# A decoder on one core: W2's butterflies moved from the experts to the second attention, and the experts' down weights split by VectorE

## The reference

```
x = x + L0_attn(layernorm(x)); x = x + L0_graph(ctx, layernorm(x))
x = x + moe(layernorm(x))               # 32 experts, capacity 256 rows
    gu  = rows_e @ w_gate_up[e]         # 256 x 512 @ 512 x 512
    act = silu(gu[:, :256]) * gu[:, 256:]
    y   = act @ w_down[e]               # 256 x 256 @ 256 x 512, gathered back per token by its gate
x = x + self_attention(layernorm(x)); x = x + cross_attention(layernorm(x), ctx)
x = x + ffn(layernorm(x))
    h   = silu(x @ W1.T) * (x @ W3.T)   # 2048 hidden features
    out = hadamard(h) @ W2.T            # Walsh-Hadamard transform over the 2048 hidden features
```

## Time and profile before

| what | value |
|---|---|
| median of 3 runs | 2982.72 us (2970.9 to 2985.78) |
| profiled execution, its own time | 2978.98 us |
| its span, first to last instruction | 2977.2 us |
| mean granted TensorE clock | 0.91 |
| busy, share of the span | PE 84%, PEld 55%, DVE 60%, ACT 41%, POOL 28% |

### The profile page before, as it was taken

How to read it: one execution, slowest core, us unless ns; L and a number is a source line. 1 busy time by engine, 2 the same in 40 slices (tenths; PEclk the granted TensorE clock), 3 DMA queues, 4 the chain that set the end, 5 groups by cost and what they waited for, 6 DMA issues and landing times. The chain is left out here.

```text
span 2977.2 us, 34561 instructions
## 1 busy us (share of the span) xinstructions
PE 2487.6 (84%) x12822; PEld 1650.5 (55%) x12822; DVE 1776.5 (60%) x2764; ACT 1224.9 (41%) x1859; POOL 833.9 (28%) x1064
## 2 busy tenths in 40 slices
PE   5898989874443458888859999999999879999999
PEld 4454545422222248778744554545655448888887
DVE  3766666636799956777736555555565444444443
ACT  3443444326767624444404333433433223333332
POOL 2222223214567637888700000001221110000000
PEclk8999999985666679999979999999999989999999
DMA  3313132203232348999842322334433432101000
GB/s 112 73 44 85 44 86 47 71 25 98 79 106 79 126 167 219 261 250 254 193 107 72 86 79 68 100 82 107 115 98 90 120 111 81 43 1 43 1 29 15
DMA packets 177289, 287.62 MB, mean 97 GB/s; under 512 B 20785, under 2 KB 52401, under 8 KB 177138
## 3 DMA queue, kind: packets, MB, share of 16 engines
q1 hardware_dynamic: 159730, 250.25, 28.4%
q0 software_dynamic: 14336, 34.61, 5.8%
q10 hardware_dynamic: 3072, 0.79, 0.1%
HBM read 149.79 MB, written 59.51 MB: 70 GB/s over the span
## 5 line engine op out<-in xcount | busy, mean ns | idle before, releaser
L657 DVE TENSOR_REDUCE at_negmax<-at_ps 128x2 f32<-128x1024 f32 (+3 forms) x256 | 259.2, 1017 | 131.2 <-PE at_ps L420 66.6
L572 ACT ACTIVATE at_probs<-at_ps 128x1024 f32<-128x1024 f32 (+3 forms) x256 | 221.8, 866 | 264.7 <-PE at_ps L440 262.1
L1258 DVE TENSOR_REDUCE a_negmax<-a_ps 128x2 f32<-128x1024 f32 x128 | 155.1, 1217 | 135.8 <-PE a_ps L1011 135.2
L50 PE MATMUL ff_ps<-ff_xnT_hi,ff_s_hi 128*128 128x512 f32 x512 | 201.0, 393 | 5.1 <-DVE ff_xnT_lo L2750 5.1
L52 PE MATMUL ff_ps<-ff_xnT_hi,ff_s_lo 128*128 128x512 f32 x512 | 200.2, 391 | 0.0
L51 PE MATMUL ff_ps<-ff_xnT_lo,ff_s_hi 128*128 128x512 f32 x512 | 200.1, 391 | 0.0
L1841 ACT ACTIVATE gr_act_signs<-gr_signed,gr_test 128x512 bf16<-128x512 f32 x248 | 177.3, 717 | 25.0 <-POOL gr_test L2204 13.4
L1159 ACT ACTIVATE a_probs<-a_ps 128x1024 f32<-128x1024 f32 x128 | 130.9, 1024 | 136.0 <-PE a_ps L1029 135.5
L2780 DVE TENSOR_TENSOR ff_hid<-ff_hid,ff_ps 128x512 f32<-128x512 f32 x64 | 44.0, 688 | 238.7 <-ACT ff_hid L2725 238.7
L440 PE MATMUL at_ps<-at_qk 98*128 98x512 f32 (+3 forms) x512 | 171.7, 417 | 17.4 <-DMA at_qk<-at_mrow 10.9
L50 PE MATMUL ex_ps<-ex_x_hi,ex_gu_hi 128*128 128x256 f32 x512 | 150.8, 294 | 35.7 <-issue 35.7
(11 more groups left out here) (411 smaller groups left out, 6503.3 us busy)
## 6 DMA issues: line engine op xcount, KB each, us to landing
at_qk<-at_part SPq DMA_DIRECT2D x384, 128.0 KB, 2.3
first_gu<-in_L_ffn_w_gate_up_dram SPq DMA_DIRECT2D x32, 1024.0 KB, 5.9
a_qk<-a_part SPq DMA_DIRECT2D x192, 128.0 KB, 2.3
first_d<-in_L_ffn_w_down_dram SPq DMA_DIRECT2D x32, 512.0 KB, 7.0
gr_aside_raw<-in_L_ffn_W_dram SPq DMA_DIRECT2D x48, 256.0 KB, 3.3
w13T<-gr_aside_out SPq DMA_DIRECT2D x32, 256.0 KB, 3.3
shared_x<-x_after_cross SPq DMA_DIRECT2D x8, 1024.0 KB, 8.0
ff_slab<-w13T SPq DMA_DIRECT2D x14, 512.0 KB, 6.9
```

The lines of the kernel that those rows point to most:

```text
L50: pe.matmul(out, lh, rh, start=start, stop=False, skip_group_check=True)
L572: act.activation(probs[:, t % 2, 2 * w:2 * w + 2, lo:S], banks(("kq", g, s), lo), ACT.Exp, scale=SCALE).then_inc(free(("kq", g, s)), 1)
L657: dve.reduce_max(negmax[:, g % 2, :].rearrange("p (j t) -> p j t", t=NT)[:, 2 * w:2 * w + 2, t], banks(("qk", g, s), 0, width(g, t)), AX.X ...
L1258: dve.reduce_max(negmax[:, g % 2, :].rearrange("p (j t) -> p j t", t=NT)[:, 2 * w:2 * w + 2, t], banks(("qk", g, s)), AX.X, negate=True).t ...
```

## The change

- The loads, butterflies and stores of W2 leave `experts`. In `attention_layers` they come back in 16 tiles of 32 columns (`MIX_COLS = HD`): at the end of SP's work of step g (g = 0 to 16) SP stores tile g-1 and loads tile g, 256 KB each in runs of 128 bytes, 2048 runs a transfer; in Pool's iteration g (1 to 16), ahead of oT(g-1), Pool does the 8 halves of tile g-1, each 128x256. `load_for_network` waits for the last store.
- `d_lo` is made by VectorE, right behind its y, and no longer by Pool.
- The order of the last two experts: both hidden parts (SiLU, h_hi; hid, h_lo) come ahead of both results on ScalarE and VectorE.

```diff
@@ attention_layers, SP
+            def load_w2(n):
+                if n:
+                    sp.wait_ge(mixed, 2 * MIX_STAGES * n)
+                sp.dma_start(mix[:, n % 2, :].rearrange("p (k c) -> p k c", c=MIX_COLS), w2_tiles[n]).then_inc(w2_in, 16)
+            def store_w2(n):
+                sp.wait_ge(mixed, 2 * MIX_STAGES * (n + 1))
+                sp.dma_start(mixed_tiles[n], mix[:, n % 2, :].rearrange("p (k c) -> p k c", c=MIX_COLS)).then_inc(w2_out, 16)
...
                 if has(g + 3):
                     stack(g + 3)
+                n = g - MIX_AT
+                if 0 <= n < MIX_TILES:
+                    store_w2(n)
+                if 0 <= n + 1 < MIX_TILES:
+                    load_w2(n + 1)
@@ attention_layers, Pool
+            def butterfly(n, stage, half):
...
+                        pool.wait_ge(w2_in, 16 * (n + 1))
+                        if n:
+                            pool.wait_ge(w2_out, 16 * n)
+                    if n or stage:
+                        pool.wait_ge(mixed, 2 * (MIX_STAGES * n + stage))
+                pool.tensor_tensor((c, d)[half], a, b, (ALU.add, ALU.subtract)[half]).then_inc(mixed, 1)
...
+                if 0 <= g - MIX_AT < MIX_TILES:
+                    for s in range(2 * MIX_STAGES):
+                        butterfly(g - MIX_AT, s // 2, s % 2)
                 if has(g - 1):
                     pool.wait_ge(rec_done, NT * g)
@@ experts, VectorE
+            def split_d(i, u):
+                d_hi_done[u].wait(dve, i, 1)
+                low(flat(d_lo[:, u]), flat(raw_d[:, u]), flat(d_hi[:, u]), d_lo_done[u])
...
+                if more:
+                    split_d(i + 1, u)
-                butterfly(e)
+            for e in range(E_ROUTED - 2):
+                hidden(e // 2, e % 2, True)
+                result(e // 2, e % 2, True)
+            for u in range(2):
+                hidden(PAIRS - 1, u, False)
+            for u in range(2):
+                result(PAIRS - 1, u, False)
@@ experts, Pool
-            split_d(0, 0)
-            split_d(0, 1)
...
-                if e + 2 < E_ROUTED:
-                    split_d(e // 2 + 1, e % 2)
```

More of the change, by code:

```diff
@@ L2258, with experts @@
 I_DIM = 256
-def experts(nc, env, tag, normed, index, target, sums, w_gate_up, w_down, w2T, w2_mixed, raw_gu, raw_d, shared_x, shared_rows):
+def experts(nc, env, tag, normed, index, target, sums, w_gate_up, w_down, raw_gu, raw_d, shared_rows):
     F = 2 * I_DIM // P
@@ L2412, in split_x, with hidden @@
                 act.copy(flat(x_hi[:, u]), flat(ps[:, 0:2, :])).then_inc(x_hi_done[u].sem, 1)
-            def body(i, u, more):
+            def hidden(i, u, more):
                 gu_ready[u].wait(act, i, 1)
@@ L2421, in body, with result @@
                     split_gu(i + 1, u)
+            def result(i, u, more):
                 y_ready[u].wait(act, i, 1)
@@ L2465, in body @@
                 dve.tensor_scalar(y[:, u, 1, :], ps[:, 7, :], gates[:, 2 * i + u, 1:2], None, ALU.mult).then_inc(y_dve[u].sem, 1)
[L2467 to L2470, removed]
-                if stage == 0 and half == 0:
-                    dve.wait_ge(w2_in, 16 * (row + 1))
-                if stage == 1 and half == 0 and row:
-                    dve.wait_ge(w2_out, 16 * row)
-                if n:
-                    dve.wait_ge(mixed, n)
-                dve.tensor_tensor((c, d)[half], a, b, (ALU.add, ALU.subtract)[half]).then_inc(mixed, 1)
+                if more:
+                    split_d(i + 1, u)
             for u in range(2):
                 split_gu(0, u)
+                split_d(0, u)
                 split_x(0, u)
-            for e in range(E_ROUTED):
-                body(e // 2, e % 2, e + 2 < E_ROUTED)
-                butterfly(e)
+            for e in range(E_ROUTED - 2):
+                hidden(e // 2, e % 2, True)
+                result(e // 2, e % 2, True)
+            for u in range(2):
+                hidden(PAIRS - 1, u, False)
+            for u in range(2):
+                result(PAIRS - 1, u, False)
         @block.gpsimd
         def _(pool):
-            def split_d(i, u):
-                d_hi_done[u].wait(pool, i, 1)
-                pool.tensor_tensor(flat(d_lo[:, u]), flat(raw_d[:, u]), flat(d_hi[:, u]).bitcast(F32), ALU.subtract
-                                   ).then_inc(d_lo_done[u].sem, 1)
             SIDE = 4
```

37 lines of the change are left out of this document (13 added, 24 removed).

## The result

The changed kernel takes 2989.16 us (median of 12 runs, 2980.8 to 2998.3). The kernel before, run beside it, takes 2974.59 us (12 runs, 2969.67 to 2985.78). The ratio is 1.0042, with a 95% interval of 1.0028 to 1.0055: slower by 0.3 to 0.6%. The forecast was 2942 us, and the result lies above its range and on the other side of no change. The profiled execution of the changed kernel took 2989.43 us, its span 2987.7 us.

A forecast was written before the change was run, and what follows sets the result against it. Pool's own program, 11.6 us an expert, was taken as the bound. Start 5, periods 31.5, end 5, less attention 1, make 40.5 us off 2978.98, 2938.5; off the median, forecast 2942 us, range 2924 to 2967.

The forecast's parts named there:

- What bounds the kernel: Experts: Pool's two gathers, two scatters, one split and four gaps make 11.6 us, taken as the 11.15 us period.
- Part 1, durations: Experts, split on VectorE: instruction lengths such as gu_lo about 2.28 us; Pool falls to 8.6 us, VectorE to about 6.5.
- Part 1, what the moved split triggers: Experts, d_lo on VectorE: little waiting for d_hi; hid(E+1), standing behind d_lo, at most 1.2 us late.
- The new period: Experts: 11.15 us falls to 10.1, bounds 9.75 and 10.8, saving 31.5 us, between 10 and 42.
- y ring: Experts: from y(E) through gathers and scatters to y(E+2), 18.8 us for two experts, 9.4 each.
- The chain of scatters: End of the experts: scatters follow one another at 7.5 us an expert, each behind the landing of the one before.
- The start: First experts: the third expert's gather comes 5.2 us earlier, saving 5 us, between 3 and 6.
- The end: Last experts: the scatters' lag goes, and SiLU moved ahead is worth at most 1.9 us; together 5 us, between 0 and 8.
- Part 3, W2 in the attention: Attention: Pool's tile takes 6.5 us, store plus load 8 us; costs 1 us in all, between 0 and 10.
- the ring at 11, landings longer in denser traffic: Experts, rival: Pool was not the bound, the period hardly moves, only the start's gain stays; about 2978 us, chance 0.06.
- The late tiles: Attention, rival: a tile's store plus load land too late for oT; slower, 3040 us at 14 us in all steps, chance 0.06.
- transfers binding: Experts, rival: transfers bind at 10.8 us an expert; 2967 us, chance 0.18.

The follow-up runs named there:

- w2_moved_only: The kernel before with only W2's butterflies and transfers moved to the attention; split still on Pool, old order of the last two experts: 2965.3 us, ratio 0.9959.
- all_but_order: The changed kernel with the old order of the last two experts: 2986.02 us, ratio 1.0019 to the kernel before.
- load_later: The changed kernel, but SP's load of an expert's weights also waits for h_lo of the expert three before: 2979.56 us, ratio 0.9998 to the kernel before.
- pair_late: The changed kernel with SP loading gate and up of e behind gu_lo(e-2), then down of e-1 right behind: 3022.78 us, ratio 1.0154 to the kernel before.
- gu_early: The changed kernel with each of SP's two loads waiting for its own split alone, gate and up behind gu_lo: 2952.79 us, ratio 0.9924 to the kernel before.

## Why the prediction was wrong

- **What bounds the kernel (Pool's own program, 11.6 us).** Probably right, but too large. The sum stands above the period that it was to explain because rows overlap: the split starts at 1304.09, while the scatter ahead of it is issued until 1304.62, and so each time. Pool's busy time is 259/300 x 11.15 = 9.6 us, with four gaps of 0.3 it is 10.8 of 11.15. `w2_moved_only` keeps all five instructions and drops to 10.66; gathers take 1.76 us there and scatters 1.62, and busy time and gaps make 10.3. So in both Pool is 0.3 to 0.4 us short of the period. That it bounds them is likely and not shown: no run takes the split off Pool and leaves the load where it was.
- **Part 1, durations.** Right: d_lo 1.23 us, gu_lo 2.29, h_lo 0.69, the copy 0.16, gathers 1.93, scatters 1.66 (forecast 1.21, 2.28, 0.7, 0.16, 1.94, 1.77). Pool has 7.1 us of instructions and 1.2 of gaps, 8.3, forecast 8.6. "Little waits there" for d_lo was a small miss: both y's now start together on a landing, and d_lo waits 0.9 us for d_hi each time.
- **Part 1, what the moved split triggers.** This is the step that failed. The prediction asked who waits behind d_lo on VectorE, and did not ask who waits for d_lo itself. SP does; its load moved from 4.5 us behind the issue of a scatter's second half to 0.3 us behind it, and the half's landing went from 6.1 us in the mean to 9.0.
- **The new period.** Its y ring carried "the landing of the second 5.6". The term is 9.8 us in the period shown and 9.0 in the mean. The chain of scatters, which the prediction itself put at 7.5 us for the end, was missing from the list of candidates; with the measured landing it is 2.64 + 9.8 + 0.1 = 12.5 us in that period, and 2.64 + 9.0 + 0.1 = 11.7 in the mean of the stretch, for a period of 11.57 over all 30. The other candidates were sized well: TensorE 254.01/300 x 11.57 = 9.80 (9.75), DMA engines 0.88 x 11.57 = 10.2 (9.6 to 10.5).
- **The start.** Right: 3.9 us from the first gather to the first y (32.98 before, 29.09 now), forecast 5 (3 to 6).
- **The end.** Nothing gained, forecast 5. The new order is worth nothing, as `all_but_order` is, if anything, ahead of the changed kernel. In the changed kernel the last scatters still wait for one another, 8.2 and 8.0 us apart, and the one of expert 30 starts 8.4 us behind its y:

```profile
1480.12 1.98 POOL L2530 DMA_INDIRECT x_after_graph<-ex_y,target  x1 [4.17 <-DMA x_after_graph<-ex_y,target]
...
1488.28 1.55 POOL L2530 DMA_INDIRECT x_after_graph<-ex_y,target  x1 [4.33 <-DMA x_after_graph<-ex_y,target]
...
1496.26 1.55 POOL L2530 DMA_INDIRECT x_after_graph<-ex_y,target  x1 [4.58 <-DMA x_after_graph<-ex_y,target]
```

- **Part 3, W2 in the attention.** Right. Eight halves take 5.9 us a tile (forecast 6.5). The pair of store and load is issued at 1631.80 and 1632.44 and lets Pool begin at 1637.29: 5.5 us (forecast 8). No row of ScalarE's copy waits for Pool there. Attention took 940.7 us in this profile, but in the profiles of the twelve kernels that have W2 there, this one included, it lies between 932.9 and 944.2, mean 937.3, against 935.8 and 935.5 without: some 2 us (forecast 1).

```profile
1631.80 0.59 SPq L377 DMA_DIRECT2D w_mixed<-shared_rows  x1
1632.44 1.21 SPq L373 DMA_DIRECT2D shared_rows<-w2T  x1
...
1637.29 5.91 POOL L783 TENSOR_TENSOR shared_rows<-shared_rows 128x256 f32<-128x256 f32 x8 [21.61 <-DMA shared_rows<-w2T]
```

- **The rivals.** The one with a chance of 0.06 was nearest: "the ring at 11, landings longer in denser traffic". Its mechanism, longer landings, is what happened; its cause was not denser traffic (the engines were less busy, 88%) but a load posted at the wrong moment, and its size was 0.6 us short. The late tiles did not happen. The one with transfers binding (0.18) did not either: DMA engines at 88% had time left.

The sum by its terms, measured in the two profiles: ahead of the experts -3.3, start -3.9, thirty periods +12.6, end +0.4, attention +4.9, together +10.7 against 10.5 in the span.

## What to carry to other kernels

When an instruction moves to another engine, list who waits for its result, DMA queues above all, and redraw where in the period their transfers are posted. Where the landing of a small transfer closes a ring, no big one should be posted while its descriptors are being written: let each load wait for its own buffer alone, and look at where in the period it then goes out. And a landing time read in the kernel before holds only for the neighbours it had there; each ring with a landing in it is worth pricing at the row's maximum too (9.2 us in the kernel before, where the median was 5.6).

## What the runs showed of the hardware

- **A load posted before a scatter's descriptors are all written delays it by 3 to 4 us, one posted just after does not.** Scatters (256 KB a half) land in 4.7 to 6.0 us without the loads (1150 to 1430 us). With 1.5 MB posted 0.3 us behind the issue (descriptors written after 1.7 us) they land in 8.2 to 9.9; in `load_later`, posted 2.3 us behind it, in 4.8 to 5.3; in `pair_late`, posted 1.2 to 1.9 us behind the start of an issue that takes 2.9, in 10.3 in the mean. Posted 2.5 us and more ahead of both halves (`gu_early`), the 1 MB costs less: they land in 6.9 and 7.2 us in the mean. The Trainium skill (DMA: Bandwidth & Descriptors, Queues, rings and completion order) says that each engine takes turns between the queue rows that have work, packet by packet. Once both queues run, from 1315.5 us in the period shown, the packets look like it. The late start does not: for 1.5 us Pool's queue moved nothing although the half's descriptors were written, and cutting the load in four, which changes no queue, took 2 us off the landing. Whether the 2 KB packets of the profile are what the page calls packets, and what decides the order at the start, was not measured.
- **gu_lo on VectorE holds up Pool's gather.** The gather issued at 1315.95 beside gu_lo took 2.90 us, and the next, with VectorE idle, 0.98. It ends 0.9 us after gu_lo does (1317.95), as if it had begun then. In `pair_late`, where gu_lo meets no gather, gathers take 1.0 us in the mean, and the scatter half beside gu_lo 2.83 instead of 1.6 (its row at 1312.10). The shorter d_lo, which began 0.9 us into the issue of a first half, did not lengthen it (1.62 us). The Trainium skill (SBUF — State Buffer, Who interferes with whom) states that an instruction of VectorE with two SBUF inputs contends with GpSimd's reads; these rows agree for the issue of an indirect DMA. The prediction took up only its inference that issue is spared, which they contradict.
- **Runs of 128 bytes were cheap.** A store and a load of 256 KB, 2048 runs each, had landed 5.5 us after the first was issued; in that stretch (1600 to 1950 us) the DMA engines are 42% busy.
- **One wait can cost twice.** The 3.9 us wait of TensorE in `load_later` was followed by a stretch at the 1.2 GHz level, all of 1304 to 1308 us, and matmuls of 512 columns that came every 0.43 us instead of 0.23.
